# Pass one of a two-layer attention kernel: q moved one turn ahead, one set of POOL operations for two normalisers, the layer's product split, the correlation's operands swapped

## The reference

```python
def autocorrelation(Q, K, V):            # 8 heads of 64 features, over 64 positions
    corr = ifft(fft(q, axis=2) * conj(fft(k, axis=2)), axis=2).real
    w, idx = top_k(corr.transpose(0, 1, 3, 2), 8)   # per feature: its 8 best lags
    w = softmax(w)
    for i in range(8):
        g = minimum(idx[..., i] + pos, L - 1)
        out = out + w[..., i] * take_along_axis(v, g, axis=2)
x = x + autocorrelation(layernorm(x), ctx, ctx)                       # pass one
x = x + (xn @ W.T + bias + lora_out), xn = layernorm(x)               # pass one
x = x + grouped-query attention of layernorm(x) over ctx              # pass two
x = x + layernorm(relu(xn @ up) ** 2 @ down + routed part)            # pass two
```

## Time and profile before

| | us |
|---|---|
| median of 3 runs | 747.17 (743.92 to 748.69) |
| profiled execution, its time | 747.23 |
| its span | 745.4 |
| busy: TensorE | 685.6 (92%) |
| busy: DVE | 495.1 (66%) |
| busy: ACT | 494.4 (66%) |
| busy: POOL | 355.5 (48%) |

### The profile page before, as it was taken

How to read it: one execution, slowest core, us unless ns; L and a number is a source line. 1 busy time by engine, 2 the same in 40 slices (tenths; PEclk the granted TensorE clock), 3 DMA queues, 4 the chain that set the end, 5 groups by cost and what they waited for, 6 DMA issues and landing times.

```text
span 745.4 us, 12189 instructions
## 1 busy us (share of the span) xinstructions
PE 685.6 (92%) x3834; PEld 475.3 (64%) x3834; DVE 495.1 (66%) x1125; ACT 494.4 (66%) x881; POOL 355.5 (48%) x445
## 2 busy tenths in 40 slices
PE   8789999999997758799999999999999999999874
PEld 4344545454553436578878878878878878876663
DVE  2687778787851875676777777677677667756421
ACT  3458686766623978687797797797787787784210
POOL 1156777765535141443553553553554554554422
PEclk8799999999999979999999999999999999999997
DMA  7224443342222211101101101101101101000000
GB/s 243 85 85 120 122 150 117 116 156 86 64 91 72 74 58 43 42 2 57 43 16 57 42 14 56 42 14 56 42 14 56 42 14 56 14 15 29 0 15 29
DMA packets 25781, 45.69 MB, mean 61 GB/s; under 512 B 3184, under 2 KB 4976, under 8 KB 25744
## 3 DMA queue, kind: packets, MB, share of 16 engines
q1 hardware_dynamic: 25744, 45.24, 19.2%
HBM read 36.84 MB, written 8.39 MB: 61 GB/s over the span
## 4 chain that ended last, share of the span: by engine, by line
PE 53%; ACT 15%; DVE 10%; issue 10%; POOL 10%; POOLq 0%; DVEq 0%; ACTq 0%
PE wide L1091 7%; PE ps_b L994 6%; ACT x L421 5%; ACT q_stack L421 5%; PE ps_b L996 5%; PE ps_b L995 5%; PE ps_b L1032 4%; PE bank L1062 4%; PE wide L1052 4%; PE ps_a L1032 4%; POOL x_res L694 3%; DVE x_in L751 2%; POOL stage L671 2%; POOL stage L674 2%; POOL rs L613 2%
## 5 line engine op out<-in xcount | busy, mean ns | idle before, releaser
L421 ACT ACTIVATE q_stack<-qt_h 32x512 fp32r<-32x512 f32 x128 | 80.6, 630 | 1.9
L611 POOL TENSOR_TENSOR va<-mv,small 128x1 f32<-128x1 f32 x80 | 15.2, 190 | 138.2 <-DVE mv L974 79.9
L691 POOL TENSOR_TENSOR y_l<-y,y_h 128x512 fp32r<-128x512 f32 x16 | 20.7, 1291 | 110.4 <-ACT y_h L553 110.4
L1091 PE MATMUL wide<-w_m,x1t 128*128 128x512 f32 x128 | 60.8, 618 | 0.7 <-ACT x1t L442 0.7
L994 PE MATMUL ps_b<-down_h,ht_h 128*128 128x512 f32 x128 | 54.1, 423 | 6.2 <-DVE ht_l L896 3.4
L903 DVE RECIPROCAL y<-ps_b 128x256 f32<-128x256 f32 x32 | 55.9, 1747 | 0.0
L994 PE MATMUL wide<-up_h,t_h 128*128 128x512 f32 x128 | 53.0, 414 | 1.2 <-DVE t_l L883 1.2
L996 PE MATMUL wide<-up_h,t_l 128*128 128x512 f32 x128 | 51.4, 401 | 0.0
L995 PE MATMUL wide<-up_l,t_h 128*128 128x512 f32 x128 | 51.1, 399 | 0.0
L996 PE MATMUL ps_b<-down_h,ht_l 128*128 128x512 f32 x128 | 51.1, 399 | 0.0
L995 PE MATMUL ps_b<-down_l,ht_h 128*128 128x512 f32 x128 | 51.0, 398 | 0.0
(11 more groups left out here) (193 smaller groups left out, 2072.8 us busy)
## 6 DMA issues: line engine op xcount, KB each, us to landing
x_in<-in_x SPq DMA_DIRECT2D x16, 256.0 KB, 2.6
ctx_t<-in_ctx SPq DMA_DIRECT2D x16, 256.0 KB, 2.6
x_res<-in_x SPq DMA_DIRECT2D x16, 256.0 KB, 2.6
x_in<-x_rows SPq DMA_DIRECT2D x16, 256.0 KB, 2.6
ctx_t<-in_ctx_turned SPq DMA_DIRECT2D x16, 256.0 KB, 2.9
x_res<-x_rows SPq DMA_DIRECT2D x16, 256.0 KB, 3.5
out<-stage SPq DMA_DIRECT2D x16, 256.0 KB, 2.0
x_rows<-x SPq DMA_DIRECT2D x8, 256.0 KB, 2.4
```

Source lines behind the costliest of these rows:

```text
L421: last = act.activation(out[STACK * part:STACK * (part + 1), p, :], halves[STACK * p:STACK * (p + 1), :].bitcast(F32), ACT.Copy)
L1091: last = pe.matmul(bank[7], cols(x1t, c, P), cols(w0_m, c, D), start=(c == 0), stop=(c == DC - 1))
```

## The change

Seven edits, all in pass one. LEAD goes from 3 to 4: tile i+4 is normalised, x is loaded for tile i+5, and q of tile i+3 is made in mid-turn, after corr. The two normalisers become one set of four POOL operations on two columns, `normalisers(i)`, for tiles i and i+4. The layer's product is a split product of three fp32r products a chunk, with `x1t_h` (a first copy on ACT) and `x1t_l` (a subtraction on POOL); the weight w0 is split the same way at the start, into the tiles of rt_h and rt_l. The correlation is 2 products with the constant `icorr` standing and prod moving, instead of 8 with prod standing; its result has lags along the partitions, so ACT copies it to `lags` and TensorE transposes it back into bank 4. ACT's exp of a tile now stands behind the two swaps.

```diff
-        LEAD = 3
+        LEAD = 4
 # SP
-                t = i + 4
+                t = i + 5
                 if live(t):
                     sp.wait_ge(S["xn1_s"], t)
                     sp.dma_start(x_in[:], rows(x_rows, t)).then_inc(S["x_loaded"], 16)
 # ACT, body(i)
                 t = i - 1
                 if live(t):
                     act.wait_ge(S["xt_ps"], t + 1)
                     wait(act, S["ffn_ps"], t)
+                    act.activation(x1t_h[:], bank[5], ACT.Copy)
+                    wait(act, S["xt_lo"], t)
                     act.activation(x1t[:], bank[5], ACT.Copy).then_inc(S["xt_s"], 1)
...
                     act.activation(cols(hi, part, PIECE), stage[n % 2][:], ACT.Copy).then_inc(S["stage_hi"], 1)
...
+                t = i + 2
+                if live(t):
+                    act.wait_ge(S["corr_ps"], t + 1)
+                    act.activation(lags[:], bank[4], ACT.Copy).then_inc(S["lag_s"], 1)
+                t = i + 3
+                if live(t):
+                    act.wait_ge(S["q_ps"], t + 1)
+                    wait(act, S["prod_s"], t)
+                    act.activation(qf[:], ps_a[:], ACT.Copy).then_inc(S["qf_s"], 1)
...
-                    act.wait_ge(S["nb2_s"], t + 1)
+                    act.wait_ge(S["nb_s"], i + LEAD + 1)
                     wait(act, S["xt_ps"], t)
...
                     act.activation(v[:, 0].rearrange("p b n -> p (b n)"), ps_b[:], ACT.Copy).then_inc(S["vf_s"], 1)
-                    act.wait_ge(S["shift_s"], t + 1)
-                    act.activation(weight[:], weight[:], ACT.Exp).then_inc(S["exp_s"], 1)
...
                     act.activation(v[0:SEQ, 1].rearrange("p b n -> p (b n)"), ps_b[SEQ:P, :], ACT.Copy)
                     act.activation(v[SEQ:P, 1].rearrange("p b n -> p (b n)"), ps_b[0:SEQ, :], ACT.Copy
                                    ).then_inc(S["vsw_s"], 1)
+                    act.wait_ge(S["shift_s"], t + 1)
+                    act.activation(weight[:], weight[:], ACT.Exp).then_inc(S["exp_s"], 1)
+                t = i + 4
+                if live(t):
+                    act.wait_ge(S["nb_s"], i + LEAD + 1)
+                    wait(act, S["q_ps"], t)
+                    act.activation(xn1[:], x_in[:], ACT.Identity, bias=nb[:, 0:1], scale=rs[:, 0:1]).then_inc(S["xn1_s"], 1)
 # ACT, peeled, i == -2
+                    for c in range(DC):
+                        act.wait_ge(S["w0_add"], c + 1)
+                        act.activation(w0_h[:, c, 0:D], w0_sum[:, c, :], ACT.Copy).then_inc(S["w0_hi"], 1)
 # POOL
+            def normalisers(i):
+                one, two = live(i + 4), live(i)
...
+                if one:
+                    pool.wait_ge(S["mv1_s"], i + 5)
+                    wait(pool, S["xn1_s"], i + 4)
+                if two:
+                    pool.wait_ge(S["mv2_s"], i + 1)
+                    wait(pool, S["xn2_s"], i)
+                pool.tensor_tensor(va[:, k], mv[:, k, 1], eps.to_broadcast([P, n]), ALU.add).then_inc(S["va_s"], 1)
+                pool.tensor_tensor(nm[:, k], mv[:, k, 0], minus.to_broadcast([P, n]), ALU.mult).then_inc(S["nm_s"], 1)
+                pool.wait_ge(S["va_s"], turn)
+                pool.tensor_tensor(rs[:, k], va[:, k], half.to_broadcast([P, n]), ALU.pow).then_inc(S["rs_s"], 1)
+                pool.wait_ge(S["rs_s"], turn)
+                pool.wait_ge(S["nm_s"], turn)
+                pool.tensor_tensor(nb[:, k], nm[:, k], rs[:, k], ALU.mult).then_inc(S["nb_s"], 1)
 # POOL, body(i), behind wgt's two operations
+                t = i - 1
+                if live(t):
+                    pool.wait_ge(S["xt_s"], t + 1)
+                    wait(pool, S["ffn_ps"], t)
+                    pool.tensor_tensor(x1t_l[:], x1t[:], x1t_h[:].bitcast(F32), ALU.subtract).then_inc(S["xt_lo"], 1)
                 n = piece_of(i)
...
                                        ).then_inc(S["stage_lo"], 1)
...
+                if live(i) or live(i + 4):
+                    normalisers(i)
                 if i == -2:
+                    for c in range(DC):
+                        pool.wait_ge(S["w0_hi"], c + 1)
+                        pool.tensor_tensor(w0_l[:, c, 0:D], w0_sum[:, c, :], w0_h[:, c, 0:D].bitcast(F32), ALU.subtract
+                                           ).then_inc(S["w0_lo"], 1)
+                if i == -1:
                     pool.wait_ge(S["bcast_in"], 16 * 7)
 # DVE
-                t = i + 3
+                t = i + 4
                 if live(t):
                     dve.wait_ge(S["x_loaded"], 16 * (t + 1))
                     dve.bn_stats(bn1[:], x_in[:]).then_inc(S["bn1_s"], 1)
...
-                    dve.wait_ge(S["corr_ps"], t + 1)
+                    dve.wait_ge(S["lag_ps"], t + 1)
 # TensorE, body(i)
                 t = i + 2
                 if live(t):
-                    pe.wait_ge(S["xn1_s"], t + 1)
-                    wait(pe, S["prod2_s"], t - 1)
-                    transform(ps_a, Q0, xn1).then_inc(S["q_ps"], 1)
                     pe.wait_ge(S["ctx_loaded"], 16 * (t + 1))
                     wait(pe, S["vsw_s"], t)
                     transform(ps_b, K0, ctx_t).then_inc(S["k_ps"], 1)
...
-                    for c in range(DC):
-                        for b in range(2):
-                            k = slice(P * c + SEQ * b, P * c + SEQ * (b + 1))
-                            last = pe.matmul(bank[4][:, k], prod[:, b, P * c:P * (c + 1)], icorr, start=True, stop=True)
+                    for b in range(2):
+                        last = pe.matmul(bank[4][SEQ * b:SEQ * (b + 1), :], icorr, prod[:, b, :], start=True, stop=True)
                     last.then_inc(S["corr_ps"], 1)
+                t = i + 3
+                if live(t):
+                    pe.wait_ge(S["xn1_s"], t + 1)
+                    wait(pe, S["prod2_s"], t - 2)
+                    transform(ps_a, Q0, xn1).then_inc(S["q_ps"], 1)
...
                     transform(ps_b, V0, ctx_t).then_inc(S["v_ps"], 1)
+                    pe.wait_ge(S["lag_s"], t + 1)
+                    for c in range(DC):
+                        last = pe.transpose(cols(bank[4], c, P), cols(lags, c, P), ident)
+                    last.then_inc(S["lag_ps"], 1)
...
-                    pe.wait_ge(S["xt_s"], t + 1)
+                    pe.wait_ge(S["xt_lo"], t + 1)
                     wait(pe, S["x2_raw"], t)
...
                     for c in range(DC):
-                        last = pe.matmul(bank[7], cols(x1t, c, P), cols(w0_m, c, D), start=(c == 0), stop=(c == DC - 1))
+                        last = split_product(bank[7], cols(x1t_h, c, P), cols(x1t_l, c, P), w0_h[:, c, 0:D], w0_l[:, c, 0:D],
+                                             c == 0, c == DC - 1)
```

More of the change, by code:

```diff
@@ L170, in build @@
         dft = one("dft", [P, DFT])
-        w0_m = one("w0_m", [P, DC * D])
+        w0_h, w0_l = rt_h, rt_l
         b0_all = one("b0_all", [P, D])
@@ L177, in build @@
         qf, prod = one("qf", [P, 2 * D]), one("prod", [P, 2, D])
+        lags = one("lags", [P, D])
         m8 = one("m8", [P, 2 * DC, TOP])
@@ L191, in build @@
         x1t = one("x1t", [P, D])
-        bn1, mv1, va1, rs1 = one("bn1", [P, 6]), one("mv1", [P, 2]), one("va1", [P, 1]), one("rs1", [P, 1])
-        nm1, nb1, nm2, nb2 = (one(n, [P, 1]) for n in ("nm1", "nb1", "nm2", "nb2"))
-        bn2, mv2, va2, rs2 = one("bn2", [P, 6]), one("mv2", [P, 2]), one("va2", [P, 1]), one("rs2", [P, 1])
+        x1t_h, x1t_l = one("x1t_h", [P, D], F32R), one("x1t_l", [P, D], F32R)
+        bn1, bn2, mv = one("bn1", [P, 6]), one("bn2", [P, 6]), one("mv", [P, 2, 2])
+        va, rs, nm, nb = (one(n, [P, 2]) for n in ("va", "rs", "nm", "nb"))
         pass1.close()
@@ L234, in build @@
             blank_s const_in dft_loaded first_in merge_in lora_in w0_in gate_in bcast_in stage_in stage_odd_in gate_split
-            coef_ready bt_ready ef_ps ef_ready w0_ps w0_add rt_ps rt_hi rt_lo
+            coef_ready bt_ready ef_ps ef_ready w0_ps w0_add w0_hi w0_lo rt_ps rt_hi rt_lo
             stage_hi stage_lo
[L237 to L240, removed]
+            nm_s nb_s va_s rs_s x_loaded ctx_loaded res_loaded bn1_s mv1_s xn1_s
+            q_ps qf_s k_ps prod_s v_ps vf_s vsw_s corr_ps lag_s lag_ps tops_s shift_s exp_s rep_s sum_s inv_s sub_s wgt_s
+            wt_ps wt_s wf_ps prod2_s o_ps x1_s bn2_s mv2_s xn2_s
+            xt_ps xt_s xt_lo ffn_ps x2_raw x2_res x2_s x2_stored x2_odd_stored""".split()
         S = {name: sem(name) for name in SEMS}
@@ L457, in body @@
                     if n == FIRST_UP:
-                        act.wait_ge(S["w0_add"], DC)
+                        act.wait_ge(S["w0_lo"], DC)
                         act.wait_ge(S["gate_split"], 2)
@@ L469, in body @@
                 if live(t):
-                    act.wait_ge(S["nb2_s"], t + 1)
+                    act.wait_ge(S["nb_s"], i + LEAD + 1)
                     wait(act, S["xt_ps"], t)
```

(22 more changed lines are left out.)

22 lines of the change are left out of this document (2 added, 20 removed).

## The result

The changed kernel takes 761.86 us (median of 5 runs, 760.71 to 768.46) against 747.17 before: ratio 1.021, interval 1.017 to 1.026: about 2 per cent slower. The forecast was 764 with a range of 753 to 774. On another chip the same kernel took 764.24 against 744.75, ratio 1.026 (1.018 to 1.034). A ratio compares all fast runs of the two kernels and is not the quotient of the two medians.

What follows compares the result with a forecast made beforehand. TensorE bounds pass one at 12.15 us a turn; after the change a 13.5 us loop through ACT, DVE and POOL does. +12.2 - 2.2 + 1.0 + 6.0 = +17.0; 745.4 + 17.0 + 1.8 gives 764 us, range 753 to 774.

Steps and rivals of the forecast that it cites:

- The loop: Pass one, nine turns with a piece: exp, DVE, POOL, xn2, vf and swaps take 13.5 us against 12.15, +12.2 us.
- TensorE's work: Pass one: shorter correlation and split layer cut TensorE's own work from 12.15 to about 10.7 us a turn.
- 13 turns of 1.42 less: Pass one: the gain if TensorE stayed the bound, 18 us, which the prediction did not believe.
- the signs that I gave: Steady turns: TensorE busy 10.4 to 10.7 of 13.5 us; ACT waits 2 for nb, DVE 2 for exp.
- Turns without a piece: Pass one, turns 10 to 13: a loop through TensorE and ACT of 11.4 us, three intervals 0.75 shorter, -2.2 us.
- The start: Start of pass one: prod(0) moves to about 13.8 and wgt(0) to 31, +6 us, with ends 3 and 10.
- The end: Last tiles of pass one: an extra copy and POOL's subtraction uncovered, the product 0.87 shorter, +1.0 us.
- My clock rival: Each turn: new TensorE idle lowers its clock, 0 to 1.5 us a turn, up to 776; 0.14 with a dearer set.
- my list of unknowns: Power of two columns, POOL subtraction price, ACT hand-overs and start: together a total of 757 to 772 us.
- TensorE remains near the bound: Pass one: all 13 turns take 11.4 us, total 744, or 738 if the start is free; 738 to 754 got 0.16.
- The swap of the correlation: Rival: the correlation's two products don't pair and take 1.9 us, costing 0.9 in four turns, 768 us; no separate chance.

Runs made afterwards that it cites:

- experiment 1: Changed kernel with POOL's set of normalisers put ahead of the piece's subtraction (stage_lo): 748.97 us against 747.16, ratio 1.005.
- 2: Changed kernel with ACT's exp back ahead of the two swaps: 765.77 us against 747.16.
- 4: Kernel before with only ACT's exp moved behind xn1 and both swaps: 757.48 us, ratio 1.017.
- 7: Changed kernel with normalisers ahead of stage_lo, w0_l's subtractions one turn later, and v directly behind q on TensorE: 750.88 us, ratio 1.007.
- 9: Changed kernel with normalisers ahead of stage_lo, w0_l one turn later, and lags' transposes directly behind wgt's: 746.60 us against 745.64, ratio 1.000.
- 8: Kernel before with the split layer alone added: 750.97 us, ratio 1.007.
- 10: Kernel before with only the correlation's operands swapped and its result copied and transposed back: 750.88 us, ratio 1.009.
- 11: Kernel before with the split layer, qf ahead of ACT's two layer copies and stage_lo behind both normaliser sets: 736.39 us against 744.45, ratio 0.991.
- 12: Kernel before with both swaps moved ahead of exp and xn1: 751.82 us, ratio 1.008.
- the repetition: The changed kernel run again unchanged, beside other variants on the same chip: 764.24 us.

## Why the prediction was right

**The loop.** Summed at 13.5 from rows, measured 13.46. Three moves on different engines changed the turn as the loop says: stage_lo out of it (experiment 1, 13.46 to 11.76, where TensorE took over), the swaps out of it (2, to 12.4), exp moved in the kernel before (4, 12.99 against 13.0). Shown. The term, +12.2, measured +12.6. That the sum hits to 0.04 is in part small errors that cancel: vf took 1.03 until the next copy and not 0.90, the set 1.23 and not 1.30, xt_lo about 1.2 and not 1.29. What was not tried alone is the merged set, and LEAD 4 with q moved.

**TensorE's work** was mis-sized: "TensorE's own work falls from 12.15 to about 10.7". It falls to 11.77. I took each instruction's price from its place in the earlier trace rows and moved it to a place with other neighbours: k, q, v and wf each 1.06 (before, two of the four 0.86), transposes 0.59 twice, the split's first product 0.43 instead of 0.23. Experiments 7 and 9 show the pairing directly. corr took 1.08 instead of 0.93 where it waited for prod. So the idle was 1.6 us a turn (0.85 ahead of k, 0.79 ahead of corr) and not 2.8, and "13 turns of 1.42 less", the gain that was there to lose, was 5 us and not 18. The forecast did not suffer, since TensorE was not in the loop that decided; what I expected of experiment 1 did. Of the signs that I gave, ACT's wait for nb was 2.02, as forecast, and DVE's wait for exp 1.06 and not 2.

**Turns without a piece**: -2.2 forecast, -2.2 measured, and that is luck. I had counted three intervals at 0.75 less, and there are four, which gave 0.55 each; 11.39 to 11.96 a turn where I had 11.4. In the one of 11.96 TensorE was full, the same mis-sizing.

**The start**: +6.0 forecast, +5.6 measured by the first xn2, with both moves where I put them: prod(0) at 14.67 (forecast 13.8), wgt(0) at 31.73 (31). But the agreement in size rests on two executions. The first xn2 came at 49.62 in one profile of the changed kernel and 47.09 in the other, and the kernel before and its variants (experiments 4, 8, 10, 11 and 12) have it anywhere from 37.41 to 44.35, the changed kernel and its variants from 45.65 to 53.06. So the start did get longer, and how much of that each cause takes is not shown; the order of the statistics ahead of prod(0) was not tried alone.

**The end**: +1.0 forecast, +4.6 in the profile and about 2.7 in the repetition. The copies and the subtraction are there; I missed that TensorE waits 2.41 us for wgt of the last tile and works at half clock behind it (0.57 and 0.50 in the two stretches above); in the repetition the same wait is 2.40 us and the clock behind it 1.00, so the wait alone does not decide it. My clock rival put the fall into every turn, where it was not: the granted clock stayed at 1.00 through all steady turns, with pauses of 0.85 and 0.79 in each. The Trainium skill, "TensorE: Matmul & The Clock Gate", section "HAM oscillation — how this bites in real kernels", says that pauses between bursts put the clock back, with an example whose pauses are longer than these. The tail agrees in one profile (2.41 us, then 0.50) and not in the other (2.40 us, then 1.00), and the short pauses of the steady turns brought no fall.

**The total.** By its terms the forecast is +17.0; the medians lie 14.7 apart, and the two profiled executions, of which the changed kernel's was its slowest, 21.3. The turns gave +10.4 where +10.0 was forecast, and that is firm. The rest, +7.0 forecast for start and end, was +10.2 in one profile and +5.8 in the other, so that 764 came so near to 761.86 is in part luck. The lower end of my list of unknowns was also added wrongly: its items give about 760, not 757.

**Rivals.** "TensorE remains near the bound" needed the set ahead of stage_lo, and experiment 1 is that kernel: 749, not my 744, by the mis-sized work. The swap of the correlation does pair: 1.08 for both products and not 1.9.

## What to carry to other kernels

When a stage is bound by one engine, write down the longest loop through the queues of the others before cutting that engine's work: each in-order queue adds all that stands between the instruction that was waited for and the one that waits. An added or moved instruction costs nothing as long as the loop is shorter than the bound, and its full length after that. Put work without a deadline (here the splitting of weights) behind whatever the next stage waits for. And price a moved instruction with its new neighbours. Read a gain of a few microseconds from the turns of the trace: start, end and total move with the granted clock.

## What the runs showed of the hardware

A transform of four 64-row passes took 1.06 us behind another kind of product and 0.86 to 0.88 behind a transform; four 128x128 transposes took 0.59 behind a transform, 0.44 to 0.45 behind transposes, the old correlation or the layer's product; the first fp32r product of a split 0.43, each further one 0.23. On POOL a power of two columns took 0.69 us and held the set's chain for 0.66, where one column took 0.55. I had forecast 0.55, with 0.36 more as the other end.
